# A graph layer on one core: records staged four units at a time, tags made relative on ScalarE

## The chip, the cores and the metric

The kernel runs on one core of a Trainium2 chip. The metric is the device time of one execution in microseconds. Before the change three runs gave 1980.95 to 1990.22 us, median 1985.97.

## What is computed

100,000 nodes with 128 features, 50,000 edges sorted by destination, 4 edge types:

```python
h = relu(layernorm(x))
for t in range(4):                       # message of an edge, by its type
    m_t = relu(concat(h[src], h[dst]) @ W1[t] + b1[t]) @ W2[t] + b2[t]
agg = segment_sum(where(edge_type == t, m_t, 0), dst)
r = sigmoid(agg @ Wir + bir + h @ Whr + bhr)
z = sigmoid(agg @ Wiz + biz + h @ Whz + bhz)
n = tanh(agg @ Win + bin + r * (h @ Whn + bhn))
out = x + (1 - z) * n + z * h
```

## The kernel before

The program is one software pipeline of 218 steps that all five engines walk through, each in its own order, with semaphores between them. A step carries work of two kinds.

**Edges.** 392 columns of 128 edges are sorted by type: a column's records (source, destination, place) are scattered to a table `lists` in DRAM, two columns (a unit) per step. Step i handles unit i + 9 of the 196 units. `stage_records` (L497 to L501) on GpSimd first copies a unit's records, 6 numbers a partition, from the big tile `records` into a slot of `stage` (8 slots), because the DMA's offsets are read there; `scatter` (L506) issues two indirect DMAs. `gather` (L513) then issues four indirect DMAs that fetch 128 rows of x each for list part q = i (204 parts). Between them stands the gate (L519), a 1x1 addition on GpSimd that all of a step's DMAs follow: its waits are for the staged copy (`l_staged`), for the rows' numbers that SyncE loaded from `lists` (`l_loaded`, L399) and for `e_normed`, by which a slot of `e_x` is free. A step of GpSimd is: copy, gate, two scatters, four gathers. SyncE loads a part's row numbers only when the scatters of the unit six further have landed.

Gathered rows get their layernorm statistics on VectorE (L799) one step later, are normalised on ScalarE seven steps after the gather (`e_h`, L998), turned and multiplied on TensorE, and end as messages with a tag: column 256 of a message holds the destination node's number (L949). ScalarE stores them to `messages` in DRAM (L1038) ten steps after the gather.

**Nodes.** 196 groups of 512 nodes. Group g is at work in steps g + 18 to g + 22. SyncE loads eight windows of 64 messages (L473) into a slot of `n_win` (4 slots), when the store of part g + 7 has landed. VectorE makes the selection matrix `n_sel` from them: four tensor_scalar operations (L906) of 128x256, each comparing node numbers with tags. TensorE sums the messages with it (L1207), ScalarE and VectorE split the sum in a high and a low part (L1077, L934), TensorE forms the gates' products (L1131 to L1133) and the rest is elementwise work: `n_r`, `n_n`, `n_zc` on ScalarE, `n_t`, `n_d`, `n_e`, `n_out` on VectorE. `n_sel` was

```python
for k in range(4):
    ins = V.tensor_scalar(n_sel[:, s % 2, k, :], iota[:], base[:, bass.ds(2 * g + k // 2, 1)],
                          n_win[:, s, k, TAG:ROW].bitcast(F32), ALU.add, ALU.is_equal)
```

with `iota` 0 to 255, `base` the first node number of each half group (392 columns, made once at L659) and the tag; both come from a tile, one number per partition.

The order in ScalarE's step is: three of four `e_h`, `n_r`, the fourth `e_h`, the store of messages, `e_ht`, `n_h_hi`, `n_a_hi`, one of four `n_h` (L1013), the store of the result and the load of x (L1051, L1030), `e_r` (L1089), two `n_h`, `n_n`, `n_zc`, one `n_h`, `e_msg`. VectorE's is: `n_out`, the message's low part (L896), `n_sel`, four statistics of edges, `n_t`, `n_xh` (L925), `n_h_lo`, `n_a_lo`, `n_t` again, four statistics of nodes (L807), the tag, `n_d`, `n_e`, with the links of a reciprocal square root between them. Each order is written out by hand in the engine's `step`; steps 0 to 31 and those from 184 are unrolled, the others run in a loop of eight.

## Time and profile before

| | before |
|---|---|
| median of 3 runs | 1985.97 us (1980.95 to 1990.22) |
| profiled execution | 1990.46 us, span 1988.6 us |
| VectorE (DVE) busy | 1791.4 us, 90% of the span |
| TensorE (PE) busy | 1748.1 us, 88% |
| ScalarE (ACT) busy | 1512.9 us, 76% |
| GpSimd (POOL) busy | 1356.8 us, 68% |
| granted TensorE clock | 0.995 |

The shares are means over stages: the first 230 us hold no node work, and scatters end near 1720 us. Busy time of GpSimd holds its DMA instructions but not the gaps between them. "issue" as what ended an idle time means that no semaphore of the profile did. An instruction's mean duration can overlap the next one's; the busy time of a group is a union.

### The profile page before, as it was taken

What the parts mean: (1) busy time and instruction counts of PE and PEld (TensorE: products, weight loads), DVE (VectorE), ACT (ScalarE), POOL (GpSimd) and SP (SyncE); (2) the same over time, 40 slices, a digit from 0 to 9 for tenths busy, and PEclk for the clock granted to TensorE, in tenths of its full rate; (3) what the DMA queues carried; (4) which work ended last, traced back from release to release, by engine and by line L of the source; (5) the groups of instructions that cost most, each with busy time, mean ns of one, the idle gap of its engine ahead of it and who ended that gap; (6) DMA issues with size and microseconds to landing.
All of it is one profiled execution on the core that took longest, in us unless ns stands there. A gap on an engine that the chain in (4) does not pass through costs nothing.

```text
span 1988.6 us, 45047 instructions
## 1 busy us (share of the span) xinstructions
PE 1748.1 (88%) x10146; PEld 1433.2 (72%) x10146; DVE 1791.4 (90%) x5325; ACT 1512.9 (76%) x3401; POOL 1356.8 (68%) x1644
## 2 busy tenths in 40 slices
PE   1015699999999999999999999999999999999898
PEld 0014477778877878788888888887887887788787
DVE  5434499999999999999999999999999999899897
ACT  0013588888888888888888888888888888788785
POOL 3777777777777777777777777777777777654300
PEclk9999999999999999999999999999999999999999
DMA  2224699988998999999999999999999999778853
GB/s 61 27 33 86 114 170 169 180 180 176 178 173 180 175 175 175 182 181 171 187 184 169 187 177 175 189 176 177 184 171 185 185 174 180 169 181 169 158 142 97
DMA packets 486059, 318.09 MB, mean 160 GB/s; under 512 B 117275, under 2 KB 472547, under 8 KB 485990
## 3 DMA queue, kind: packets, MB, share of 16 engines
q1 hardware_dynamic: 185286, 106.73, 37.6%
q10 hardware_dynamic: 261792, 156.12, 28.4%
q0 software_dynamic: 38912, 54.48, 16.1%
q14 instruction: 46, 0.38, 0.1%
q8 instruction: 23, 0.38, 0.1%
HBM read 211.39 MB, written 105.71 MB: 159 GB/s over the span
## 4 chain that ended last, share of the span: by engine, by line
PE 31%; POOL 27%; issue 15%; DVE 11%; DMA 5%; ACT 2%; SPq 1%; ACTq 1%; POOLq 0%; DVEq 0%
POOL e_x L513 16%; POOL lists L506 8%; PE bank L1131 6%; PE bank L1132 5%; PE bank L1133 5%; PE bank L1207 5%; DVE n_sel L906 3%; DMA n_win<-messages 2%; PE bank L1236 2%; DMA messages<-e_msg 2%; POOL gate_word L519 2%; PE bank L1218 2%; PE bank L1219 2%; PE bank L1246 2%; SPq L473 1%
## 5 line engine op out<-in xcount | busy, mean ns | idle before, releaser
L513 POOL DMA_INDIRECT e_x<-in_x,rows_now x816 | 826.2, 1012 | 253.1 <-issue 252.8
L506 POOL DMA_INDIRECT lists<-stage x392 | 402.2, 1026 | 144.8 <-issue 144.7
L998 ACT ACTIVATE e_h<-e_x,shift,rstd 128x128 f32<-128x128 f32 x816 | 354.0, 487 | 120.9 <-DVE shift L883 120.9
L1013 ACT ACTIVATE n_h<-n_x,shift,rstd 128x128 f32<-128x128 f32 x784 | 360.7, 487 | 0.0
L906 DVE TENSOR_SCALAR n_sel<-iota,base,n_win 128x256 fp32r<-128x256 f32 x784 | 275.0, 412 | 18.7 <-DMA n_win<-messages 18.5
L799 DVE BATCH_NORM_STATS2 bn<-e_x 128x6 f32<-128x128 f32 x816 | 175.9, 275 | 126.0 <-DMA e_x<-in_x,rows_now 125.3
L1207 PE MATMUL bank<-n_sel,n_win 128*128 128x256 f32 x1568 | 239.8, 296 | 45.3 <-DVE n_sel L906 43.4
L1131 PE MATMUL bank<-n_h_hi,whh_hi 128*128 128x512 f32 x588 | 248.3, 422 | 13.2 <-ACT n_zc L1101 5.6
L1207 PEld LDWEIGHTS bank<-n_sel,n_win 128*128 128x128 f32 x1568 | 199.3, 190 | 82.2 <-DVE n_sel L906 69.7
L1131 PE MATMUL bank<-n_a_hi,wih_hi 128*128 128x512 f32 x588 | 249.3, 424 | 0.0
L1133 PE MATMUL bank<-n_a_hi,wih_lo 128*128 128x512 f32 x588 | 233.4, 397 | 0.0
L1132 PE MATMUL bank<-n_a_lo,wih_hi 128*128 128x512 f32 x588 | 233.1, 396 | 0.0
L1133 PE MATMUL bank<-n_h_hi,whh_lo 128*128 128x512 f32 x588 | 232.3, 395 | 0.0
L1132 PE MATMUL bank<-n_h_lo,whh_hi 128*128 128x512 f32 x588 | 232.3, 395 | 0.0
L1187 PE MATMUL bank<-ident,e_h 128*128 128x128 f32 x816 | 127.8, 281 | 115.7 <-ACT e_h L998 114.8
L1077 ACT ACTIVATE n_a_hi<-bank 128x512 fp32r<-128x512 f32 x196 | 117.2, 598 | 144.4 <-PE bank L1207 136.1
L1089 ACT ACTIVATE e_r<-bank,b_cols 128x128 f32<-128x128 f32 x408 | 127.6, 364 | 108.8 <-DVE n_xh L925 55.2
L1187 PEld LDWEIGHTS bank<-ident,e_h 128*128 128x128 f32 x816 | 105.3, 145 | 142.4 <-issue 115.2
L1218 PE MATMUL bank<-e_ht,w 128*128 128x128 f32 x816 | 165.2, 286 | 34.4 <-DVE e_msg L896 30.9
L807 DVE BATCH_NORM_STATS2 bn<-n_x 128x6 f32<-128x128 f32 x784 | 167.9, 273 | 0.0
L1219 PE MATMUL bank<-e_ht,w 128*128 128x128 f32 x816 | 164.8, 285 | 0.0
L1218 PEld LDWEIGHTS bank<-e_ht,w 128*128 128x128 f32 x816 | 131.0, 200 | 37.5 <-issue 37.5
(141 smaller groups left out, 3879.4 us busy)
## 6 DMA issues: line engine op xcount, KB each, us to landing
n_win<-messages SPq DMA_DIRECT2D x1568, 64.2 KB
messages<-e_msg ACTq DMA_DIRECT2D x204, 257.0 KB
n_x<-in_x ACTq DMA_DIRECT2D x195, 256.0 KB
out<-n_out ACTq DMA_DIRECT2D x195, 256.0 KB
e_x<-in_x,rows_now POOLq DMA_INDIRECT x816
lists<-stage POOLq DMA_INDIRECT x392
rows_now<-lists SPq DMA_DIRECT2D x204, 2.0 KB
w<-in_W SPq DMA_DIRECT2D x1, 512.0 KB
```

What stands on the lines that cost most here:

```text
L506: G.indirect_dma_start(lists, bass.IndirectOffsetOnAxis(ap=stage[:, s, k, 2:3], axis=0), stage[:, s, k, 0:2], None).then_inc(l_scattered[s ...
L513: G.indirect_dma_start(e_x[:, s, 2 * end + t, :], None, x, bass.IndirectOffsetOnAxis(ap=rows_now[:, s, t, end:end + 1], axis=0)).then_inc( ...
L906: ins = V.tensor_scalar(n_sel[:, s % 2, k, :], iota[:], base[:, bass.ds(2 * g + k // 2, 1)], n_win[:, s, k, TAG:ROW].bitcast(F32), ALU.add ...
L998: last = A.activation(e_h[:, s % 2, k, :], e_x[:, s, k, :], ACT.Relu, scale=rstd[:, slot, col + k:col + k + 1], bias=shift[:, slot, col + ...
L1013: last = A.activation(n_h[:, s % 2, cols], n_x[:, s, cols], ACT.Relu, scale=rstd[:, slot, col + 4 + k:col + 5 + k], bias=shift[:, slot, co ...
L1131: T.matmul(o, w_hi, v_hi, start=start, stop=False)
L1132: T.matmul(o, w_hi, v_lo, start=False, stop=False)
L1133: return T.matmul(o, w_lo, v_hi, start=False, stop=stop)
L1187: last = T.transpose(bank[BE0][:, k * P:(k + 1) * P], e_h[:, s, k, :], ident[:])
L1207: last = T.matmul(o, n_win[:, w, k, part_ * D:(part_ + 1) * D], n_sel[:, s, k, :], start=n == 0, stop=n == 3)
L1218: T.matmul(o, w1[:, kind, 0, :], e_ht[:, s, t * P:(t + 1) * P], start=True, stop=False)
L1219: last = T.matmul(o, w1[:, kind, 1, :], e_ht[:, s, (2 + t) * P:(3 + t) * P], start=False, stop=True)
```

## The change

Two edits. GpSimd copies four units' records in one copy of 24 numbers a partition, into four slots, at the end of a step behind its gathers, in one step of four (and 0 and 4 ahead of the first scatter, 8 behind the first scatters); the gates of the other steps no longer wait for `l_staged`. In the loop the copy has no wait for earlier scatters of its slots. And ScalarE makes `n_rel` = tag - base at the head of its step, two activations of two columns, which takes over the wait for the windows (`n_windowed`); VectorE waits for `n_reled` and compares `iota` with `n_rel` alone. `base` is now made negative once. Nothing else is changed.

```diff
+        n_rel = sb("n_rel", [P, 2, 4])
...
             def stage_records(u, m):
                 s = m % UNROLL
-                if due(u - 7):
-                    pool.wait_ge(l_scattered[s], uses(u - 8, s, UNROLL, 32))
-                G.tensor_copy(stage[:, s, :, :], records[:, bass.ds(2 * u, 2), :]).then_inc(l_staged, 1)
+                if isinstance(u, int) and u >= UNROLL:
+                    for k in range(4):
+                        pool.wait_ge(l_scattered[s + k], uses(u - 8 + k, s + k, UNROLL, 32))
+                G.tensor_copy(stage[:, s:s + 4, :, :].rearrange("p u k c -> p (u k) c"),
+                              records[:, bass.ds(2 * u, 8), :]).then_inc(l_staged, 4)
...
-            for u in range(scatters_before(0)):
+            for u in (0, 4):
                 stage_records(u, u)
             for u in range(scatters_before(0)):
-                pool.wait_ge(l_staged, u + 1)
+                if u % 4 == 0:
+                    pool.wait_ge(l_staged, u + 4)
                 scatter(u, u)
+            stage_records(8, 8)
...
             def step(i, m):
-                for u, k in units:
-                    stage_records(u, k)
...
                 for u, k in units:
-                    pool.wait_ge(l_staged, u + 1)
+                    if k % 4 == 0:
+                        pool.wait_ge(l_staged, u + 4)
                 transfers_may_start(i + 1)
                 for u, k in units:
                     scatter(u, k)
                 if within(i, UNITS):
                     gather(i, m)
+                for u, k in units_of(i + 1, m + 1):
+                    if k % 4 == 0 and due(u - 7):
+                        stage_records(u, k)
...
-                link(V.tensor_copy(base[:], base_i[:]))
+                V.tensor_scalar(base[:], base_i[:], -1.0, None, ALU.mult).then_inc(s_bases, 1)
...
-                    dve.wait_ge(n_windowed[s], uses(g, s, 4, 128))
+                    dve.wait_ge(n_reled, g + 1)
...
-                        ins = V.tensor_scalar(n_sel[:, s % 2, k, :], iota[:], base[:, bass.ds(2 * g + k // 2, 1)],
-                                              n_win[:, s, k, TAG:ROW].bitcast(F32), ALU.add, ALU.is_equal)
+                        ins = V.tensor_scalar(n_sel[:, s % 2, k, :], iota[:], n_rel[:, s % 2, k:k + 1], None, ALU.is_equal)
...
             def step(i, m):
+                g, s = i - LAG + 1, (m - LAG + 1) % 4
+                if within(g, NG):
+                    if isinstance(g, int) and g == 0:
+                        act.wait_ge(s_bases, 1)
+                    act.wait_ge(n_windowed[s], uses(g, s, 4, 128))
+                    if due(g - 1):
+                        act.wait_ge(n_seled, g - 1)
+                    for half in range(2):
+                        rows = slice(2 * half, 2 * half + 2)
+                        last = A.activation(n_rel[:, s % 2, rows], n_win[:, s, rows, TAG].bitcast(F32), ACT.Identity,
+                                            bias=base[:, bass.ds(2 * g + half, 1)])
+                    last.then_inc(n_reled, 1)
                 normalise_edges(i, m, (0, 1, 2))
```

GpSimd's order in steps of its loop was, one step after the other:

```order
L501 COPY stage<-records 128x6 [waits l_scattered5]
L519 TENSOR_TENSOR gate_word<-g_power 1x1 [waits l_staged,l_gated,e_normed,l_loaded4]
L506 DMA lists<-stage 102400x2 x2
L513 DMA e_x<-in_x,rows_now 128x128 x4
L501 COPY stage<-records 128x6 [waits l_scattered6]
L519 TENSOR_TENSOR gate_word<-g_power 1x1 [waits l_staged,l_gated,e_normed,l_loaded5]
```

and is now:

```order
L507 COPY stage<-records 128x24 [waits l_scattered6,l_scattered5,l_scattered7,l_scattered4]
L526 TENSOR_TENSOR gate_word<-g_power 1x1 [waits l_staged,l_gated,e_normed,l_loaded3]
L513 DMA lists<-stage 102400x2 x2
L520 DMA e_x<-in_x,rows_now 128x128 x4
L526 TENSOR_TENSOR gate_word<-g_power 1x1 [waits l_gated,e_normed,l_loaded4]
L513 DMA lists<-stage 102400x2 x2
L520 DMA e_x<-in_x,rows_now 128x128 x4
L526 TENSOR_TENSOR gate_word<-g_power 1x1 [waits l_gated,e_normed,l_loaded5]
```

The copy of three gates is gone, and with it their wait for `l_staged`; in front of the fourth a copy of 24 numbers still stands, with nothing between it and the gate.

ScalarE's order from the end of one step into the next (ISA is a register operation on its queue) was:

```order
L1108 ACTIVATE e_msg<-bank 128x2x128 [waits e_tagged,e_messaged]
L987 ISA
L998 ACTIVATE e_h<-e_x,shift,rstd 128x128 [waits e_turned,ln_ops]
L998 ACTIVATE e_h<-e_x,shift,rstd 128x128 x2
L1061 ACTIVATE n_r<-bank,bsum 128x512 [waits n_ted,n_gate_r]
L998 ACTIVATE e_h<-e_x,shift,rstd 128x128 [waits ln_ops]
L1038 ISA [waits e_low]
L1038 DMA messages<-e_msg 128x2x257
```

and is now:

```order
L1131 ACTIVATE e_msg<-bank 128x2x128 [waits e_tagged,e_messaged]
L1070 ISA
L1075 ISA [waits n_seled,n_windowed0]
L1075 ACTIVATE n_rel<-n_win,base 128x2
L1075 ISA
L1075 ACTIVATE n_rel<-n_win,base 128x2
L998 ISA
L1009 ACTIVATE e_h<-e_x,shift,rstd 128x128 [waits e_turned,ln_ops]
L1009 ACTIVATE e_h<-e_x,shift,rstd 128x128 x2
L1084 ACTIVATE n_r<-bank,bsum 128x512 [waits n_ted,n_gate_r]
```

The wait for the windows stands ahead of all of ScalarE's step, and two activations with it.

## Rows read from the trace of the kernel before

**Rows 1.** Stretches: time, busy us (x instructions) by engine, clock, DMA share, GB/s
```profile
900.00:1650.00 750.00, 736.40 (x4349) 603.71 (x4348) 742.36 (x2217) 644.08 (x1447) 572.81 (x681) 1.00 0.94 180
1730.00:1825.00 95.00, 92.95 (x554) 76.61 (x554) 93.47 (x283) 81.59 (x184) 46.41 (x55) 1.00 0.76 178
```

**Rows 2.** Grouped lines, 900 to 1650 us: count, busy us, mean ns, idle before
```profile
L906 DVE TENSOR_SCALAR n_sel<-iota,base,n_win 128x256 fp32r<-128x256 f32 x340 | 119.5, 413 | 0.0
L1089 ACT ACTIVATE e_r<-bank,b_cols 128x128 f32<-128x128 f32 x170 | 53.2, 364 | 44.5 <-DVE n_xh L925 27.3 <-issue 17.2
L1077 ACT ACTIVATE n_a_hi<-bank 128x512 fp32r<-128x512 f32 x86 | 51.4, 598 | 54.4 <-PE bank L1207 53.8 <-issue 0.6
L1108 ACT ACTIVATE e_msg<-bank 128x256 fp32r<-128x256 f32 x85 | 31.5, 371 | 0.0
L519 POOL TENSOR_TENSOR gate_word<-g_power 1x1 f32<-1x1 f32 x85 | 30.6, 359 | 13.2 <-POOL stage L501 12.3
L501 POOL COPY stage<-records 128x6 int32 x86 | 28.0, 326 | 0.4
```

**Rows 3.** Waits, 400 to 1700 us: who, for whom, us, times, longest
```profile
POOL gate_word L519 <- ACT e_h L998: 6.8, 4, 2.9
DVE n_sel L906 <- DMA n_win<-messages: 5.8, 4, 2.4
...
DVE bn L799 <- DMA e_x<-in_x,rows_now: 0.2, 1, 0.2
```

**Rows 4.** Waits, 0 to 300 us
```profile
DVE bn L799 <- DMA e_x<-in_x,rows_now: 123.8, 18, 30.0
```

**Rows 5.** Timeline of GpSimd ahead of the loop: start, duration, instruction
```profile
27.85 2.12 POOL L501 COPY stage<-records 128x6 int32<-128x6 int32 x7 [24.69 <-DVE records L644]
30.15 1.49 POOL L506 DMA_INDIRECT lists<-stage  x1 [0.17 <-POOL stage L501]
...
180.49 0.19 POOL L501 COPY stage<-records 128x6 int32<-128x6 int32 x1
180.92 0.19 POOL L519 TENSOR_TENSOR gate_word<-g_power 1x1 f32<-1x1 f32 x1 [0.24 <-POOL stage L501]
...
189.42 0.18 POOL L519 TENSOR_TENSOR gate_word<-g_power 1x1 f32<-1x1 f32 x1 [0.24 <-POOL stage L501]
```

**Rows 6.** Grouped lines of VectorE, 3 to 5 us
```profile
L608 DVE CAST iota<-iota_i 128x256 f32<-128x256 int32 x1 | 0.3, 295 | 0.0
L609 DVE TENSOR_SCALAR above_r<-iota,part 128x128 fp32r<-128x128 f32 x1 | 0.3, 285 | 0.0
...
L610 DVE CAST ones_r<-ones 128x128 fp32r<-128x128 f32 x1 | 0.2, 220 | 0.0
```

**Rows 7.** Timeline of a step of the loop, all engines
```profile
1012.54 0.39 ACTq L1038 DMA_DIRECT2D messages<-e_msg  x1
...
1014.89 0.20 POOL L501 COPY stage<-records 128x6 int32 x1
...
1015.25 0.82 POOL L519 TENSOR_TENSOR gate_word<-g_power 1x1 f32<-1x1 f32 x1 [0.17 <-POOL stage L501]
...
1016.84 5.27 SPq L473 DMA_DIRECT2D n_win<-messages  x8
...
1018.86 0.98 POOL L513 DMA_INDIRECT e_x<-in_x,rows_now  x1 [0.30 <-issue]
...
1019.90 1.26 ACT L998 ACTIVATE e_h<-e_x,shift,rstd 128x128 f32<-128x128 f32 x3
...
1021.13 1.37 DVE L906 TENSOR_SCALAR n_sel<-iota,base,n_win 128x256 fp32r<-128x256 f32 x4
...
1021.38 0.38 ACTq L1038 DMA_DIRECT2D messages<-e_msg  x1
```

**Rows 8.** The chain of waits, 520 to 580 us: start, duration, what
```profile
540.43 7.41 DMA messages<-e_msg
...
553.11 6.08 DMA n_win<-messages
```

More of the change, by code:

```diff
@@ L279, in gnn_layer @@
         s_edges_ready = sem("s_edges_ready")
+        s_bases = sem("s_bases")
         g_blank = sem("g_blank")
@@ L333, in gnn_layer @@
         n_xhed = sem("n_xhed")
+        n_reled = sem("n_reled")
         n_seled = sem("n_seled")
@@ L548, in _, with units_of @@
             pool.wait_ge(s_spots, 1)
-            for u in range(scatters_before(0)):
+            for u in (0, 4):
                 stage_records(u, u)
             for u in range(scatters_before(0)):
-                pool.wait_ge(l_staged, u + 1)
+                if u % 4 == 0:
+                    pool.wait_ge(l_staged, u + 4)
                 scatter(u, u)
+            stage_records(8, 8)
             pool.wait_ge(s_iota, 1)
             G.tensor_tensor(gate_word[:, 0:1], g_power[0:1, 0:1], g_power[0:1, 0:1], ALU.add).then_inc(l_gated, 1)
+            def units_of(i, m):
+                if not isinstance(i, int):
+                    return [(i + LEAD, m + LEAD)]
+                return [(u, u) for u in range(scatters_before(i), min(scatters_before(i + 1), SCATTERS))]
             def step(i, m):
-                units = []
-                if not isinstance(i, int):
-                    units = [(i + LEAD, m + LEAD)]
-                else:
-                    units = [(u, u) for u in range(scatters_before(i), min(scatters_before(i + 1), SCATTERS))]
-                for u, k in units:
-                    stage_records(u, k)
+                units = units_of(i, m)
                 if within(i, UNITS):
```

## The prediction

> **What bounds the kernel now.** I read the stretches first. From 900 to 1650 us VectorE is busy 742.4 of 750 us and TensorE 736.4; ScalarE has 644.1 and GpSimd 572.8 [rows 1]. A count of the grouped lines turns this into steps: 85 gates of GpSimd in that stretch, so 750/85 = 8.82 us a step, and VectorE is busy 8.73 of them [rows 1, 2]. The waits from 400 to 1700 us say whose busy time is real: VectorE waits for a window of messages 4 times (5.8 us) and once for gathered rows (0.2 us) in some 147 steps, so it waits for nobody [rows 3]. TensorE's busy time is modelled and proves less. When the scatters end, GpSimd falls to 46.4 of 95 us and VectorE still has 93.5 [rows 1]: VectorE's own work sets the step there, not what GpSimd takes from it.
>
> GpSimd looks free by its busy time and is not. In its sequence nearly each DMA instruction has 0.30 us in front of it that no semaphore ends (the gather at 1018.86 [rows 7]); I take that as part of the instruction. It waits for e_normed, its only brake, 4 times (6.8 us) [rows 3]. So it also works through its 8.82 us. Two engines are level, and a change on one alone would give little. Before 300 us GpSimd leads alone: VectorE waits 123.8 us for gathered rows, 18 times [rows 4], and a step takes 189.42 - 180.92 = 8.50 us [rows 5].
>
> **VectorE: a pointer scalar less.** n_sel is 128x256, two [P,1] operands, 413 ns, four a step [rows 2]. What the second pointer costs no row tells alone. Without a pointer a 128x128 cast takes 220 ns, with one a 128x128 tensor_scalar takes 285: 65 ns for a pointer; without one 128x256 takes 295 [rows 6]. One pointer on 256 columns would then be 360, against 413 for two, and the second would cost 53; were the two equal, 59. From below: 0, if both are loaded together and 413 is 295 plus one lot of 118. From above: 413 - 295 = 118, if what is left costs nothing. I take 57, between these two. 4 x 57 = 0.23 us a step; of it I count 0.22, since such ops overlap. VectorE's step goes from 8.82 to 8.60. The constant's sign (a tensor_scalar in place of a cast, once) costs nothing that counts: it is done before VectorE waits for its first gathers.
>
> The Trainium skill (VectorE: DVE Perf Modes, the TRN2 errata) gives a VectorE op on SBUF as 58 cycles and the columns over the mode's factor, with no term for pointers. By it n_sel costs the same with one as with two, this term is 0 and the time is that of the rival of the free pointer; the 285 ns on 128 columns beside 295 on 256 speak against it.
>
> **GpSimd: three copies of four go.** In the steady stretch copy and the wait behind it are 28.0 + 13.2 us over 85 steps, 0.48 a step; undisturbed they are 0.36 (1014.89 to 1015.25) [rows 2, 7]. Before the loop they are 0.43 (180.49 to 180.92) [rows 5]. What takes their place in a step without a copy is the gate right behind a DMA, 0.05 at a guess between 0 and 0.30. I take 0.36 saved in three steps of four, 0.27 a step. In the fourth, the copy still stands directly in front of its gate (nothing lies between "behind the gathers" and the next step's head), and has 24 columns for 6: saving 0. The copy's waits for four scatters hold nothing: they are four to eight steps old. Seven copies before the first scatter, 2.12 us and 0.17 [rows 5], become two, and a third stands behind the first scatters: 1.2 us saved. GpSimd's step: 8.82 - 0.27 = 8.55, and 8.50 - 0.28 at the start.
>
> **ScalarE: two small activations at the head.** A pair of e_r with a bias pointer is 53.2/85 = 0.63 us for 128 columns [rows 2]; two columns must be less, and it can't be below 0. An n_a_hi of 512 columns takes 598 ns and an e_msg of 256 takes 371 [rows 2], 0.89 ns a column, so 126 columns fewer leave about 0.15 of each half of the 0.63; with a step's register work I take 0.35 for both. ScalarE idles before n_a_hi and e_r 54.4 + 44.5 us over 85 steps, 1.16 a step [rows 2]; that is the cover, and without it 0.35 would be on the path. The Trainium skill (ScalarE: Activation LUTs, what ACT_TABLE_LOAD costs) makes it 188 ns apiece, 0.38 for both: the cover holds by either.
>
> What waits now at ScalarE's head is n_windowed, and behind it e_h, n_r, the store of messages and e_ht are queued; VectorE waits for n_reled as it did for the window. The head is 1.23 us before n_sel (1019.90 against 1021.13) [rows 7], so windows have that much less time. In the trace a store issued at 1012.54 lets SyncE go at 1016.84, and its eight loads take 5.27 us, to 1022.11; the ScalarE head that needs them comes at 1019.90 + 8.82 = 1028.7 [rows 7]. That leaves 6.6 us for landing; shorter steps and the later store take 0.8 of it, 5.8. A late load took 6.08 us after a store of 7.41 [rows 8]. So now and then the head waits; I give 3 us back in all for it.
>
> **The sum.** Steady: 192 of the 196 steps with node work x 0.22 = 42 us. Start, where GpSimd leads: 17 of the first 23 steps have no copy, x (0.43 - 0.05) = 6, and 1.2: 7 us. Back: 3. Together 46 less. The profiled execution took 1990.5 us (span 1988.6), the median run 1986.0, so I start from their middle, 1988.2: **1942 us**. Against the profiled time alone it would be 1944.5, against the median 1940.
>
> **Rivals.**
> *GpSimd becomes the bound (chance 0.21).* If only 0.17 a step goes on average, because what VectorE's operations block is blocked elsewhere (a gate took 0.82 us at 1015.25 under n_xh, where 0.18 is usual [rows 5, 7]), GpSimd's step is 8.65 to 8.70 and VectorE waits for gathers at last. 0.14 x 192 = 27, and 6: 1988 - 33 = 1955. For it: it is level now. Against: n_sel holds less long. The Trainium skill (SBUF — State Buffer, who interferes with whom) says that a tensor_scalar in a two-port mode locks GpSimd out for the whole instruction, and that two SBUF inputs block its reads; the gate of 0.82 us under an addition of two SBUF tiles agrees.
>
> *The second pointer is free (0.12).* Then VectorE keeps 8.82, and only the start is gained: 1981. For it: only 128-column ops show what a first pointer costs, none a second. This is also how the change would fail to do what it says.
>
> *The window becomes the bound at ScalarE's head (0.07): slower.* The store goes out 1.48 us behind the head (1019.90 to 1021.38 [rows 7]), 1.83 with the two activations. The head of two steps on waits for it, so a step is at least (trip + 1.83)/2, the trip being store issue to last landing. Here it is 4.30 + 5.27 + landing; with 6.08 it is 15.65 and the step 8.74, hidden under 8.82 but not under 8.60. From a mean trip of 15.9 (step 8.87) the kernel is slower than before. DMA queues are 94% busy at 180 GB/s [rows 1], and a faster step loads them more; at 16.1 the step is 8.97, and 0.15 x 192 = 29, less 7 of the start: 1988 + 22 = 2010. Against: VectorE waited for windows four times in 147 steps.
>
> **How the numbers follow.** The forecast has 0.60. Its own range is 1925 to 1960: the low end takes 0.29 a step (n_sel at 340 ns, and less blocking) and gives nothing back, the high end 0.14. GpSimd as the bound lies in it or just above. The range, 1922 to 1982, takes in the free pointer and leaves out the window rival and a gain from the full 118 ns. 0.5%, 10 us, is what a measurement can tell from no change. Faster by over that (below 1976): forecast, GpSimd rival, and a little of the rest, 0.81. Within: the free pointer and a mild window case, 0.12. Slower: 0.07.
>
> **What the profile after would show.** n_sel at 350 to 360 ns; VectorE still busy 99% with 8.6 us from gate to gate. If n_sel is at 400 or more, the VectorE term is wrong. Copies of 128x24, some 49, right in front of every fourth gate, and other gates within 0.1 us of the last gather. If VectorE's bn waits for gathers in the steady stretch, GpSimd is the bound. If ScalarE shows tens of us of waits for n_win at n_rel, and VectorE then waits for n_rel, it is the window; the prediction is wrong if those waits pass 20 us, or if the step isn't below 8.7.

## The result and the profile after

The changed kernel takes 1962.6 us in the median of six runs (1955.7 to 1973.0), the kernel before 1981.7 us in the median of six (1979.9 to 1990.2). The ratio is 0.9897, with a 95% interval of 0.987 to 0.9924: about 1.0% faster, 19 us. The prediction said 46 us. The profiled execution took 1973.0 us, the longest of the six, with a span of 1971.2; I compare it with the profiled one of before (1990.5, span 1988.6, also the longest of its six), 17.4 us apart. In what follows, a ratio with an interval compares undisturbed runs only, while a median is that of all runs.

Busy time and a group of instructions from the page of the changed kernel (columns as in the rows ahead of the prediction):

```profile
PE 1735.8 (88%) x10146; PEld 1436.8 (73%) x10146; DVE 1768.0 (90%) x5325; ACT 1545.4 (78%) x3793; POOL 1307.9 (66%) x1497
...
L918 DVE TENSOR_SCALAR n_sel<-iota,n_rel 128x256 fp32r<-128x256 f32 x784 | 248.9, 379 | 24.2 <-ACT n_rel L1075 23.7
```

The two stretches of [rows 1], for the changed kernel:

```profile
900.00:1650.00 750.00, 729.36 (x4328) 603.50 (x4327) 731.57 (x2202) 654.35 (x1613) 544.47 (x615) 1.00 0.90 179
1730.00:1825.00 95.00, 93.44 (x551) 77.71 (x550) 92.15 (x286) 83.75 (x206) 42.80 (x52) 0.98 0.77 174
```

VectorE has lost 10.8 us of busy time in 750 and stands idle for 18.4 us there instead of 7.6 [rows 1]. The grouped lines of the same stretch, which answer to [rows 2]:

```profile
L526 POOL TENSOR_TENSOR gate_word<-g_power 1x1 f32<-1x1 f32 x85 | 17.8, 210 | 34.8 <-ACT e_h L1009 31.0 <-POOL stage L507 3.3
L507 POOL COPY stage<-records 128x24 int32 x21 | 4.5, 216 | 0.1
...
L1112 ACT ACTIVATE e_r<-bank,b_cols 128x128 f32<-128x128 f32 x170 | 53.1, 364 | 43.6 <-DVE n_xh L936 24.6 <-issue 17.5 <-PE bank L1242 1.2
L1100 ACT ACTIVATE n_a_hi<-bank 128x512 fp32r<-128x512 f32 x85 | 50.8, 597 | 37.8 <-PE bank L1230 36.9 <-issue 0.8
...
L1075 ACT ACTIVATE n_rel<-n_win,base 128x2 f32<-128x2 f32 x170 | 40.7, 290 | 13.7 <-DMA n_win<-messages 13.6
...
L1131 ACT ACTIVATE e_msg<-bank 128x256 fp32r<-128x256 f32 x85 | 31.5, 371 | 0.0
```

GpSimd's copies and gates now cost 22.3 us instead of 58.6 [rows 2], but what it gained it waits out: its gate waits 31.0 us for ScalarE's e_h. The waits from 400 to 1700 us, against [rows 3]:

```profile
POOL gate_word L526 <- ACT e_h L1009: 52.5, 75, 4.0
...
ACT n_rel L1075 <- DMA n_win<-messages: 27.4, 13, 3.6
...
DVE n_sel L918 <- ACT n_rel L1075: 14.7, 10, 2.8
```

Windows were waited for 4 times (5.8 us) before [rows 3] and are 13 times now (27.4 us), at ScalarE's head, and half of that reaches VectorE. Such a trip in the chain of waits (start, duration, what), beside [rows 8]:

```profile
1068.13 7.40 DMA messages<-e_msg
...
1080.30 6.55 DMA n_win<-messages
```

And the start, in GpSimd's timeline, against [rows 5]:

```profile
27.88 0.77 POOL L507 COPY stage<-records 128x24 int32<-128x24 int32 x2 [24.71 <-DVE records L656]
28.82 1.53 POOL L513 DMA_INDIRECT lists<-stage  x1 [0.17 <-POOL stage L507]
...
154.42 0.21 POOL L507 COPY stage<-records 128x24 int32<-128x24 int32 x1
154.88 0.18 POOL L526 TENSOR_TENSOR gate_word<-g_power 1x1 f32<-1x1 f32 x1 [0.24 <-POOL stage L507]
155.57 1.03 POOL L513 DMA_INDIRECT lists<-stage  x1 [0.52 <-issue]
...
162.09 1.02 POOL L520 DMA_INDIRECT e_x<-in_x,rows_now  x1 [0.30 <-issue]
163.14 0.18 POOL L526 TENSOR_TENSOR gate_word<-g_power 1x1 f32<-1x1 f32 x1
163.48 1.01 POOL L513 DMA_INDIRECT lists<-stage  x1 [0.16 <-POOL gate_word L526]
...
170.84 0.18 POOL L526 TENSOR_TENSOR gate_word<-g_power 1x1 f32<-1x1 f32 x1
```

A step without a copy takes 170.84 - 163.14 = 7.70 us, against 8.50 [rows 5]. The copy and its wait are gone (0.43), and so is most of the pause behind the gate (0.36 of 0.52): the first scatter comes 0.16 us behind a gate that waited for nothing, 0.52 behind one that waited. The first row operation (n_sel) stands at 220.7 us instead of 233.3.

**Where the 17.4 us come from.** I took the start of each step's first n_sel from both traces. The first is 12.6 us earlier, the last 17.2 (1954.6 against 1971.8). So the start gave 12.6 us, the 195 steps behind it 4.5, and the rest 0.2. The 4.5 are not spread evenly: the 17th n_sel group stands at 361.4 us against 381.8, a lead of 20.3 us, and from there to the last the changed kernel loses 3 us again. Behind 382 us it gained nothing in these two executions. The steps of a calm stretch repeat in eights:

```
step time us, first n_sel to first n_sel, eight steps of a calm stretch          mean
before  8.43  8.91  9.01  8.75  8.49  9.01  9.02  8.75                            8.80
after   8.39  8.91  8.78  8.68  8.59  8.99  8.83  8.68                            8.73
```

Calm steps are only 0.07 us shorter (70.37 against 69.85 for the eight), where 0.22 was predicted. Over all 195 steps, those up to 9.2 us last 8.77 us in the mean before (181 of them) and 8.66 after (171), which gives 21.7 us; the longer ones exceed that mean by 28.3 us together before (14) and by 45.4 after (24), which takes back 17.1. So there are two questions: why is the calm step hardly shorter, and are the long steps a cost of the change?

The long steps, sorted by what VectorE waits for in them: those with a wait of n_sel for its windows, and the ones right behind them, make up 21.9 us before (12 steps) and 28.8 after (17), 6.9 more. The rest are 6.4 us before (2 steps) and 16.7 after (7), 10.3 more. Five of these seven follow each other from 1679.7 to 1738 us, without a wait for windows. There VectorE waits for TensorE's and ScalarE's results, and the granted clock is 0.88:

```profile
1679.00:1738.00 59.00, 49.41 (x261) 41.16 (x261) 44.46 (x136) 41.41 (x101) 25.68 (x31) 0.88 0.65 149
```

The kernel before has one such step, of 14.3 us at 1698.6. Whether the change has a part in these five is not shown.

### The profile page after: what moved, and what is told of

The parts are those of the page before. It is cut to its first block, busy times and chain, and to the rows that moved or that the text cites. A ratio compares the mean times of both kernels' runs of the same rounds, so it can differ in the third digit from the quotient of the medians.

```text
span 1971.2 us, 45215 instructions
## 1 busy us (share of the span) xinstructions
PE 1735.8 (88%) x10146; PEld 1436.8 (73%) x10146; DVE 1768.0 (90%) x5325; ACT 1545.4 (78%) x3793; POOL 1307.9 (66%) x1497
## 4 chain that ended last, share of the span: by engine, by line
PE 49%; DVE 16%; DMA 9%; issue 8%; ACT 4%; SPq 3%; POOL 2%; ACTq 1%; DVEq 0%; POOLq 0%
PE bank L1154 9%; PE bank L1156 8%; PE bank L1155 8%; PE bank L1230 7%; DMA messages<-e_msg 5%; DMA n_win<-messages 4%; DVE n_sel L918 4%; PE bank L1259 4%; SPq L476 3%; PE bank L1241 3%; PE bank L1242 3%; PE bank L1269 2%; DVE bn L811 2%; PE bank L1210 2%; PE bank L1255 2%
## 5 line engine op out<-in xcount | busy, mean ns | idle before, releaser
L513 POOL DMA_INDIRECT lists<-stage x392 | 410.9, 1048 | 141.9 <-issue 139.5
L918 DVE TENSOR_SCALAR n_sel<-iota,n_rel 128x256 fp32r<-128x256 f32 x784 | 248.9, 379 | 24.2 <-ACT n_rel L1075 23.7
L1154 PE MATMUL bank<-n_h_hi,whh_hi 128*128 128x512 f32 x588 | 248.8, 423 | 17.4 <-ACT n_zc L1124 8.8
```

Of the source, the lines that this page charges most:

```text
L513: G.indirect_dma_start(lists, bass.IndirectOffsetOnAxis(ap=stage[:, s, k, 2:3], axis=0), stage[:, s, k, 0:2], None).then_inc(l_scattered[s ...
L918: ins = V.tensor_scalar(n_sel[:, s % 2, k, :], iota[:], n_rel[:, s % 2, k:k + 1], None, ALU.is_equal)
L1154: T.matmul(o, w_hi, v_hi, start=start, stop=False)
```

## What holds the calm step

From 1356 to 1636 us both traces are calm. The stretch, first before, then after (columns as in [rows 1]):

```profile
1356.00:1636.00 280.00, 275.07 (x1624) 225.09 (x1623) 277.33 (x827) 240.18 (x542) 211.41 (x255) 1.00 0.94 180
```

```profile
1356.00:1636.00 280.00, 273.49 (x1631) 225.90 (x1630) 275.46 (x831) 245.82 (x607) 204.29 (x231) 1.00 0.91 181
```

VectorE's n_sel in it, before and after:

```profile
L906 DVE TENSOR_SCALAR n_sel<-iota,base,n_win 128x256 fp32r<-128x256 f32 x127 | 44.9, 415 | 0.0
```

```profile
L918 DVE TENSOR_SCALAR n_sel<-iota,n_rel 128x256 fp32r<-128x256 f32 x128 | 42.1, 390 | 1.3 <-ACT n_rel L1075 1.3
```

In busy time (operations overlap) four n_sel are 4 x 44.9/127 = 1.41 us before and 4 x 42.1/128 = 1.32 after, 0.10 a step. (The 1.3 us of waiting are one wait, in a single long step.) Yet the operation itself is as short as predicted. The query of one line (duration minimum, median and maximum), from 900 to 1650 us, before and after:

```profile
L906 DVE TENSOR_SCALAR n_sel<-iota,base,n_win x340: 394/406/639, 906.6 to 1647.2; 128x256 fp32r<-128x256 f32 x170
```

```profile
L918 DVE TENSOR_SCALAR n_sel<-iota,n_rel x340: 333/347/562, 901.9 to 1645.6; 128x256 fp32r<-128x256 f32 x170
```

The median is 347 ns against 406, but the mean is 388 against 413: some operations are much longer than the rest. I set against each other when GpSimd's DMA instruction ends and how long the n_sel under way takes. In a timeline of the changed kernel:

```profile
1364.18 1.35 DVE L918 TENSOR_SCALAR n_sel<-iota,n_rel 128x256 fp32r<-128x256 f32 x4
...
1364.46 0.96 POOL L520 DMA_INDIRECT e_x<-in_x,rows_now  x1 [0.30 <-issue]
...
1365.70 0.18 POOL L526 TENSOR_TENSOR gate_word<-g_power 1x1 f32<-1x1 f32 x1 [0.28 <-ACT e_h L1009]
```

The last gather ends at 1365.42, the fourth n_sel at 1365.53, 0.11 us behind it; it took 551 ns. At 347 ns it would have ended 0.2 us earlier. Counted over all n_sel between 300 and 1900 us (worked out from the traces: the first end of a GpSimd DMA instruction behind the start of the n_sel, and how much longer than 413 or 346 ns the n_sel took):

```
DMA instruction ends      before (two pointers)      after (one pointer)
behind the start of       n_sel   over 30   mean     n_sel   over 30   mean
the n_sel by              met     ns more   extra    met     ns more   extra
0 to 250 ns                27       0        -6        8       0         0
250 to 300                 81       0        -6        2       2       +45
300 to 350                 23      14       +34       29      29      +100
350 to 400                 23      23       +71       31      31      +141
400 to 450                  5       5      +114       81      81      +201
450 to 500                  4       4      +168        3       2      +150
```

This is the shape of a wait: an n_sel whose own end falls near the end of a GpSimd DMA instruction ends some 110 ns behind it, and where its own end comes well before, it loses nothing. In the changed kernel all 143 met between 250 and 450 ns are late, in the kernel before all 28 met between 350 and 450. That 81 met between 250 and 300 lose nothing before fits too: the end of the DMA instruction and 110 ns is still under 413. Summed, such meetings cost 24 us after and 4 us before. That is 20 us over 180 steps, 0.11 a step, half of what the shorter operation should have given.

The steps up to 9.2 us between 400 and 1680 us close the sum (worked out from the traces, means in us):

```
                                   before   after   difference
step                                8.80    8.71       0.09
first n_sel's start to the          1.40    1.30       0.10
  fourth one's end
the same where no n_sel is late     1.37    1.13       0.24
```

So of 0.24 us, 0.14 go to late n_sel, and all the rest of the step is as long as before (7.40 us in both).

Other operations of VectorE serve as a control. Between 300 and 1900 us of the changed kernel, 60 n_sel have the end of a GpSimd DMA instruction within 90 ns ahead of to 50 ns behind the place where they would end undisturbed, and all 60 are late. 88 of the layernorm statistics and 57 n_a_lo have one there as well, and none is late: of the 1424 statistics none takes over 291 ns, with medians of 271 and 272. So the wait belongs to n_sel and not to VectorE as a whole.

Why are there more of them? Not because GpSimd has moved under n_sel. Between 300 and 1700 us a GpSimd DMA instruction ends 1.13 to 1.29 us behind the step's first n_sel in 82 of 158 steps before, and in 107 of 158 after. One of the 82, from the step of [rows 7], whose first n_sel starts at 1021.13:

```profile
1021.42 0.95 POOL L513 DMA_INDIRECT e_x<-in_x,rows_now  x1 [0.30 <-issue]
```

It ends at 1022.37, 1.24 us behind, and the four n_sel take 407 to 408 ns. What has moved is n_sel's own end. With two pointers the fourth runs from 0.97 to 1.38 us behind the first one's start, past 1.2 + 0.11. With one it would run from 0.80 to 1.14, and it ends at 1.30 in the median. The shorter operation draws its end to where the DMA instruction's end was all along. GpSimd's wait for e_h (the next gate comes 1.5 us behind the first n_sel in the median, 2.9 before) changes which gather lies there, the last one after and the one before it in the step shown. Why a DMA instruction ends there so often in both kernels is not shown.

## The experiments

Two theories were put down with the runs. **A**: the row operation waits for the end of GpSimd's DMA instruction, and this gives back VectorE's gain. **B**: the wait for windows, now at ScalarE's head, gives it back.

At about 1980 us neither half of the change was measured alone. Most runs came out in a condition that the first measurement did not have: on four chips the kernel before itself took 2639 to 2713 us in the median. Each is compared with the kernel before of its own set, but of the change at 1980 us these say little; they have a part of their own below. One set, on a fifth chip, came near the first measurement (the kernel before at 2021.6 us) and is told first.

### The light kernels: TensorE relieved, before and after

```diff
             def product(o, w_hi, w_lo, v_hi, v_lo, start, stop):
-                T.matmul(o, w_hi, v_hi, start=start, stop=False)
-                T.matmul(o, w_hi, v_lo, start=False, stop=False)
-                return T.matmul(o, w_lo, v_hi, start=False, stop=stop)
+                return T.matmul(o, w_hi, v_hi, start=start, stop=stop)
```

The same edit in the kernel before (l0) and in the changed one (l1). Expected of l0:

> The kernel before with TensorE relieved: each gate's product is its first matmul alone, so 12 of the 18 matmuls of 128x512 of a step are left out and with them the low parts of the product (part of the computation is left out). It tests two things. First, that the runs of 2640 to 2710 us were long because TensorE's results came late: every unexplained wait there stands before an operation that reads one of TensorE's banks. If so, this kernel takes 1900 to 2000 us although the kernel before takes 2600 us or more beside it; if the memory or the queues were slow, it takes 2400 us or more as well. Second, it is the base for the other light kernels: VectorE's 413 ns row operations and its step of 8.6 to 8.8 us hold it.

Expected of l1:

> The changed kernel with TensorE relieved in the same way (12 of 18 gate matmuls of a step left out). Against the light kernel before, if VectorE bounds both: with the row operations free of GpSimd the step would fall by the whole 0.24 us, to about 8.5, and the time by 45 to 60 us with the start. Theory A (a row operation that meets the end of a GpSimd DMA instruction waits for it) says that part of it is given back as in the full kernel: 60 or more delayed row operations between 900 and 1650 us, each ending some 110 ns behind the end of a GpSimd DMA instruction, calm step only 0.05 to 0.15 lower, 15 to 40 us in all. Theory B (the waits on windows at ScalarE's head) says calm steps lower by 0.2 and more, and the loss in single long steps behind a wait of ScalarE on windows.

**Measured.** l0 2026.0 us (2014.3 to 2041.3, 4 runs), l1 2003.4 us (1983.6 to 2020.7, 10 runs), the kernel before 2021.6 us (1984.4 to 2062.9, 13 runs). l0 is 1.0125 of the kernel before (0.993 to 1.032), l1 1.0006 (0.994 to 1.007); the light change from l0 to l1 is 22.6 us by the medians, in the 15 to 40 that theory A gave. With TensorE's busy time down to 523.6 of 750 us, l0 is no faster within its interval, and its calm steps are those of the kernel before. TensorE does not bound these steps, for all its 98% of busy time [rows 1]. The calm eight of l0 are 8.43, 8.90, 8.99, 8.74, 8.49, 8.97, 9.00, 8.75, those of the kernel before to 0.04; those of l1 are those of the changed kernel.

Theory A's count came out: 69 n_sel of l1 took over 50 ns too long between 900 and 1650 us (86 in the changed kernel) and lost 10.7 us, in the median 112 ns behind the end of a DMA instruction of GpSimd; 11 in l0, 0.9 us. Yet in l0 the next gate comes 1.6 us behind the first n_sel, nearly as early as in the changed kernel. So an early gate alone does not make n_sel late; the short operation does. The first n_sel stands at 221.1 us against 231.8: the start again, 10.7 us.

These two traces also hold a control. Behind 1790 us the scatters have ended, GpSimd's last gather is done over 2.6 us ahead of the next gate, and no DMA instruction ends near the end of an n_sel. The line query on five calm steps of l0, then of l1:

```profile
L906 DVE TENSOR_SCALAR n_sel<-iota,base,n_win x20: 403/406/411, 1815.2 to 1851.1; 128x256 fp32r<-128x256 f32 x20
```

```profile
L918 DVE TENSOR_SCALAR n_sel<-iota,n_rel x20: 342/347/350, 1800.4 to 1835.2; 128x256 fp32r<-128x256 f32 x20
```

No n_sel is late (at most 411 and 350 ns), and the steps are 8.31, 8.97, 8.88, 8.74 in l0 and 8.07, 8.73, 8.68, 8.50 in l1: 0.23 us a step, the whole of the predicted 0.22. Where the two engines do not meet, the step falls by what the operation lost. So the predicted term is real, and in the steady stretch meetings take back over half of it. (GpSimd has less to do there in other ways too, as its scatters are over.) The changed kernel's own stretch behind 1750 us reads the same, with four steps of 8.74, 8.68, 8.50 and 8.07 us against 8.44, 8.97, 8.88 and 8.75 in the kernel before, 0.26 a step:

```profile
L918 DVE TENSOR_SCALAR n_sel<-iota,n_rel x24: 342/345/348, 1754.8 to 1798.3; 128x256 fp32r<-128x256 f32 x24
```

Theory B is not gone with that. On this chip windows were late more often in both kernels. From 400 to 1700 us, first l0, then l1:

```profile
DVE n_sel L906 <- DMA n_win<-messages: 41.4, 19, 5.1
```

```profile
ACT n_rel L1075 <- DMA n_win<-messages: 78.2, 39, 5.9
...
DVE n_sel L918 <- ACT n_rel L1075: 46.6, 26, 4.9
```

The number of waits doubled, and yet VectorE lost about the same to them (46.6 against 41.4 us), and the steps over 9.2 us exceed the mean of the others by 93 us in l1 against 84 in l0. The earlier wait costs something, some 5 to 10 us here, and not the gain of the calm step, which B would have left at 0.2.

### Half of the change alone, n_sel moved, GpSimd shifted

Copies alone (the subtraction stays in n_sel), cut to its core:

```diff
-                    dve.wait_ge(n_reled, g + 1)
+                    dve.wait_ge(n_windowed[s], uses(g, s, 4, 128))
...
-                        ins = V.tensor_scalar(n_sel[:, s % 2, k, :], iota[:], n_rel[:, s % 2, k:k + 1], None, ALU.is_equal)
+                        ins = V.tensor_scalar(n_sel[:, s % 2, k, :], iota[:], base[:, bass.ds(2 * g + k // 2, 1)],
+                                              n_win[:, s, k, TAG:ROW].bitcast(F32), ALU.add, ALU.is_equal)
```

> The copies of four units alone; n_sel with two pointers and base on VectorE as before. Theory A (a VectorE operation of n_sel that meets the end of a GpSimd DMA instruction waits for it; GpSimd, being faster, is now held by e_normed at a fixed place where its last gather meets n_sel): first n_sel 12 us earlier than before, gates wait for e_h in the loop, the fourth n_sel is longer than the others by 50 ns or more, the loop's step is 8.79 to 8.95 as before or longer; 1970 to 1985 us. Theory B (the wait for windows at ScalarE's head takes the gain; port meetings don't matter): step 8.79, few waits for windows, 1972 to 1976 us.

Subtraction alone (one copy in front of each gate, as before):

```diff
-                for u, k in units_of(i + 1, m + 1):
-                    if k % 4 == 0 and due(u - 7):
-                        stage_records(u, k)
...
+                for u, k in units:
+                    stage_records(u, k)
```

> ScalarE's subtraction alone; copies as before. Theory A: no gain at the start, n_sel about 346 ns with few operations delayed as in the kernel before (GpSimd has no slack and so is not held at one place), step 8.60 to 8.70 in calm stretches unless GpSimd becomes the bound; 1955 to 1975 us. Theory B: n_rel waits for windows 25 us or more between 400 and 1700 us as in the changed kernel, and the total is 1980 or more.

All four n_sel behind the edge statistics (late), and two of the four there (split):

```diff
+                last = None
+                if within(i - 1, UNITS):
+                    last = edge_stats(i - 1, m - 1)
                 g, s = i - LAG + 1, (m - LAG + 1) % 4
                 if within(g, NG):
                     dve.wait_ge(n_reled, g + 1)
```

> The changed kernel with n_sel behind the four statistics of edges on VectorE, 0.8 us later in the step. Theory A: operations of n_sel no longer meet the last gather's end; delayed ones fall from 86 in 750 us to under 40, and the step falls by 0.1 unless TensorE, which gets n_sel later, becomes the bound; 1940 to 1965 us. Theory B: VectorE's waits for n_rel fall, ScalarE's for windows stay; no other change, 1955 to 1962 us.

```diff
-                    for k in range(4):
+                    for k in (0, 1):
...
+                if within(g, NG):
+                    for k in (2, 3):
+                        ins = V.tensor_scalar(n_sel[:, s % 2, k, :], iota[:], n_rel[:, s % 2, k:k + 1], None, ALU.is_equal)
+                    ins.then_inc(n_seled, 1)
```

> The changed kernel with two of the four n_sel ahead of the statistics of edges and two behind them, and TensorE starting on the first half. The end of the last gather falls in the statistics, which do not use the port. Theory A: nearly no delayed n_sel, calm step 8.73 to 8.60, 1935 to 1955 us. Theory B: as the changed kernel, 1958 to 1966 us.

Three of them were repeated, since the kernel before itself was slow beside them:

> Only the copies of four units on GpSimd; the tags' subtraction stays in VectorE's operation with two pointers. The same kernel as e1_copies, run again because the kernel before itself took some 2700 us beside e1_copies, so that no part of the change could be read there. What is expected with the kernel before at about 1980 us: the start is shorter by the whole 12 us (first row operation of L914's place at 221 us instead of 233), and the steady step stays at about 8.79, since VectorE keeps its 413 ns operations and holds it. Both theories give 1968 to 1975 us, ratio 0.993 to 0.997.

> Only ScalarE's subtraction and VectorE's operation with one pointer; GpSimd copies one unit before each gate as before. The same kernel as e2_rel, run again for the same reason. Theory A (the shorter operations meet the end of a GpSimd DMA instruction): GpSimd's step of 8.50 and more now leaves still less room below VectorE's, so GpSimd's gates and DMA instructions lie against the row operations as they do in the changed kernel or closer: step 8.70 to 8.80, 1970 to 1982 us, ratio 0.994 to 1.000. Theory B (the wait for windows at ScalarE's head takes the gain, the calm step is 8.60): waits of ScalarE on windows of 25 us and more and a calm step of 8.65 or less, 1965 to 1975 us.

> Only ScalarE's subtraction and VectorE's operation with one pointer; GpSimd copies one unit before each gate as in the kernel before. The same kernel as e2_rel. The first row operation should stand at 231 to 234 us, as in the kernel before, since the start is GpSimd's. Theory A: GpSimd's DMA instructions lie against the row operations as closely as in the changed kernel, calm step 8.68 to 8.80, 40 or more delayed operations; with a start that gains nothing the ratio to the kernel before is 0.994 to 1.002. Theory B: calm step 8.65 or less and waits of ScalarE on windows of 25 us and more, ratio 0.988 to 0.995. Against the changed kernel's 0.990, the difference is what the copies of four units bring.

> The changed kernel with two of the four row operations of VectorE moved behind the next edge statistics. The same kernel as e4_split, run again because the kernel before itself took some 2700 us beside it. With the kernel before at about 1980 us, theory A: two of the four operations lie elsewhere against GpSimd's DMA instructions, so the fourth is no longer met by the last gather in each step: fewer than 60 delayed operations between 900 and 1650 us (86 in the changed kernel) and a calm step of 8.60 to 8.70, 1945 to 1960 us. Theory B: the waits on windows stay at some 25 us, the step stays at 8.7, 1958 to 1970 us.

> The changed kernel with two of the four row operations of VectorE moved behind the next edge statistics; the same kernel as e4_split, now hoped for beside a kernel before of about 1980 to 2020 us (on the chip of the light kernels the kernel before took 2021.6 us). Theory A: the fourth operation is no longer met by the last gather in each step: fewer than 60 delayed operations between 900 and 1650 us (86 in the changed kernel), calm step 8.60 to 8.70 instead of 8.73, and 0.5 to 1.5% below the changed kernel's 0.990 of the kernel before, so a ratio of 0.975 to 0.985. Theory B: waits on windows decide, the calm step is 8.73 or the same within 0.03, ratio 0.987 to 0.995.

And GpSimd's DMA instructions shifted against VectorE:

```diff
+                pool.wait_ge(l_gated, i + 1)
+                for n in range(2):
+                    G.tensor_tensor(pad[:, n:n + 1], g_power[0:1, 0:1], g_power[0:1, 0:1], ALU.add)
                 transfers_may_start(i + 1)
```

> The changed kernel with two small GpSimd additions of one element (some 0.19 us each) before each gate, which move GpSimd's eight DMA instructions of a step 0.4 to 0.5 us later against VectorE's operations; nothing else changes. With the kernel before at about 1980 us: theory A (a row operation that meets the end of a GpSimd DMA instruction waits for it) says that the calm step changes, because other row operations are met: 8.60 to 8.75 if the last gather now ends behind the four row operations or between them and another, and operations are delayed at other positions than the fourth; GpSimd's own sequence takes about 0.45 us a step more and still fits under 8.7. Theory B (waits for windows at ScalarE's head) says no change of the calm step, 8.73, and the same ends within 0.3%. If the kernel before takes some 2700 us again, TensorE's late results bound every step, GpSimd waits several us in most steps, and both theories say no difference from the changed kernel.

**Measured**, each beside the kernel before of its own set (medians in us; without an interval the ratio is that of the medians):

```
                    this      before    this/before
copies alone      e1  2709.8    2697.5    1.005
                  e1b 2730.7    2712.9    1.007
subtraction alone e2  2611.4    2697.5    0.9705  (0.961 to 0.980)
                  e2b 2611.3    2712.9    0.955   (0.940 to 0.970)
                  e2c 2562.7    2655.1    0.968   (0.953 to 0.984)
n_sel late        e3  2776.0    2697.5    1.033   (1.023 to 1.042)
n_sel split       e4  2649.9    2697.5    0.982
                  e4b 2554.1    2639.0    0.973   (0.963 to 0.983)
                  e4c 2539.3    2655.1    0.962   (0.953 to 0.972)
GpSimd shifted    e5  2567.9    2639.0    0.973
```

None of these expectations' times could be put to the test, since all assumed 1980 us. Of their counts, those of the late and split kernels came out (4, and 7 to 12 delayed n_sel), and the 40 or more of the subtraction alone did not (22 to 35). What the sets say is this.

**The condition itself.** Steps take 11 to 13 us, the granted clock from 900 to 1650 us is 0.86 to 0.91 in the mean (1.00 is the level of 2.4 GHz, 0.5 that of 1.2) instead of 1.00 in [rows 1], and all engines pause. A stretch of e2c (columns as in [rows 1]):

```profile
900.00:1650.00 750.00, 599.03 (x3236) 488.14 (x3237) 553.11 (x1649) 494.67 (x1205) 411.54 (x506) 0.91 0.76 133
```

Its waits from 400 to 1700 us:

```profile
POOL gate_word L522 <- ACT e_h L1000: 354.2, 94, 10.3
ACT n_r L1075 <- remote: 133.9, 52, 3.5
...
PE bank L1221 <- DVE n_sel L909: 68.9, 29, 4.6
DVE n_out L895 <- remote: 68.1, 30, 4.1
...
ACT n_rel L1066 <- DMA n_win<-messages: 6.5, 2, 4.2
```

"Remote" is a release that the trace cannot assign. In each of the ten traces of this condition, from 300 to 1900 us, it stands before n_r, n_out, n_t, n_zc, e_msg, e_r, e_ht, n_a_hi and n_h_hi and before nothing else, and each of these reads a bank that TensorE has written; in the traces of before and after the change and in the light ones it does not occur. That points at TensorE's results coming late, by up to 10.4 us; what held them the trace does not tell. The light kernels were to show whether TensorE is the cause, but beside them the kernel before took 2021.6 us: the condition was not there, and the test not made. The lower clock alone is not enough: from 1023.7 to 1031 us in e2b the granted clock is 1.00, the gate matmuls start 0.23 us apart, and n_r then waits 1.7 us all the same (waits of e2b, 1030 to 1033 us):

```profile
ACT n_r L1075 <- remote: 1.7, 1, 1.7
```

The cause stays open.

**What the parts do there.** TensorE waits for n_sel 46 to 91 us between 400 and 1700 us in each of these traces, against 21.4 in the kernel before at 1990 us. Where it waits, n_sel would be on the path, and its time would count in another way; this is argued from the waits and not tested. The subtraction alone gains 3 to 4.5%; all four n_sel moved behind 0.86 us of statistics lose 3%, against the subtraction alone some 0.8 us a step ((2776 - 2611)/196); and the copies alone gain nothing that can be seen, as they relieve an engine that waits 455 us for e_h anyway (e1b, 400 to 1700 us). So in that condition the gain that was measured is the subtraction's; the changed kernel itself was not run there.

**What they say on A.** The late kernel moves n_sel away from the last gather. From 900 to 1650 us, by the same line query:

```profile
L922 DVE TENSOR_SCALAR n_sel<-iota,n_rel x236: 333/346/524, 900.6 to 1647.5; 128x256 fp32r<-128x256 f32 x118
```

Four of these 236 took over 50 ns too long; in the split kernel 7 to 12 did, and where n_sel stayed in its place (e2, e2b, e2c, e5) 22 to 35. The ends again lie some 105 to 115 ns behind the DMA instruction in the median. In e2c all 54 n_sel met between 300 and 450 ns behind their start were late, by 110, 145 and 207 ns in the three slots of the table, as in the changed kernel (100, 141, 201), though the two kernels keep quite another pace. That supports A's mechanism. The shifted GpSimd (e5) tells nothing on the calm step it was made for, as there was none: 22 of its n_sel were late, as in e2. Which place of n_sel is best at 1980 us was not tried: the split kernel is no better than the subtraction alone in the first set (2650 against 2611) and ahead by less than the spread of the runs in the third (2539 against 2563).

## Why the prediction was wrong in its size

The direction was right, and 1962.6 us lies in the range, but the forecast of 1942 (its own range 1925 to 1960) missed by 20 us. That it lies in the range is partly luck: the start gained 5.6 us more than predicted, while the steps behind it gained far less.

- **VectorE's term, 42 us, is the step that failed.** The size of the operation was right: 347 ns in the median where 350 to 360 stood, the second pointer 59 ns. What failed is "of it I count 0.22" a step: that the whole of a shorter operation reaches the step. Steps up to 9.2 us fell by 0.09 between 400 and 1680 us, since 0.14 of the 0.24 goes to n_sel waiting for the end of GpSimd's DMA instructions. Over all 195 steps it was 0.11 a step, 21.7 us where 42 were forecast. Where nothing meets, the full 0.23 shows.
- **GpSimd's start, 7 us, was 12.6.** The term mis-sized is the saving in a step without a copy: 0.38 predicted, 8.50 - 7.70 = 0.80 measured, because the pause behind the gate fell as well (0.52 to 0.16), which no row of before could show, each gate there having waited, for a copy or, at the end, for e_normed. The 1.2 us of the first copies came as 2.12 - 0.77 = 1.35. By 17 such steps and the first copies it would be 15 us, and the gate of the 23rd step does stand 15.5 us earlier (242.4 against 257.9).
- **GpSimd's steady term** took nothing from the end, as predicted: the gate's wait for e_h went from 6.8 us [rows 3] to 52.5.
- **ScalarE's cost** was 40.7/85 = 0.48 us busy a step, for 0.35 predicted. The prediction's own figures give more than it took: half of 0.63 less 126 columns of 0.89 ns is 0.20 for each activation, not 0.15. The idle time in front of n_a_hi and e_r fell from 98.9 [rows 2] to 81.4 us, and the rest of the calm step did not grow, so it was covered.
- **Windows, 3 us back**, were 27.4 us of waits at ScalarE's head, over the 20 that the prediction named as proving it wrong, and 14.7 at VectorE. The step did not come below 8.7 in the mean either, the other such sign: 8.73 in the calm eight, 8.84 from 900 to 1650 us with the long ones. In steps longer than 9.2 us the windows cost 6.9 us more than before, and the two light kernels put it at 5 to 10. The rival itself (the window holds each step, 2010 us) did not come: the calm step never waits.
- **No term at all** stood for the other long steps: 10.3 us more than before in these two executions, mostly the five from 1679.7 us. Their cause stays open. With it the sum closes: 12.6 + 21.7 - 6.9 - 10.3 = 17.1, and the last n_sel stands 17.2 us earlier.
- **Rival "GpSimd becomes the bound"** gave 1955 us by its number and fails by its mechanism: VectorE never waits for gathers in the steady stretch. Its reason was that the engines block each other. They do, but what took the gain is VectorE's side of it. The gate of 0.82 us at 1015.25 [rows 7] was the other direction; gates are 210 ns in the mean after, 359 before [rows 2]. The Trainium skill (SBUF — State Buffer, who interferes with whom) says that whichever of the two issues first gets the shared pair of ports for its whole instruction, and the other blocks. The trace agrees that VectorE can be the one that waits, but not on the whole instruction: an n_sel met by the end of a DMA instruction of 0.95 us within 250 ns of its start ran under it and lost nothing (0 of 8 late after, 0 of 27 before).
- **Rival "the second pointer is free"** is out: 347 against 406 ns. The formula of the Trainium skill (VectorE: DVE Perf Modes, TRN2 errata) has no term for pointers, and by it the two would cost the same; the trace does not agree.

## What to carry to other kernels

When two engines run level, a saving on one is not free of the other: before counting it, look for what ends near the place where the shortened instruction will end. Compare the median and the mean of an operation's duration; a mean well over the median (347 and 388 here) says that some wait inside, and the time since the neighbour's last end says for what. And a busy share proves a bound only with the waits: TensorE at 98% was no bound of the calm step, as taking two thirds of its gate matmuls away showed.

## What was not expected of the hardware

- An n_sel of VectorE whose own end falls near the end of a GpSimd DMA instruction ends about 110 ns behind it, losing up to some 200 ns; one that ends earlier loses nothing, and of 1424 statistics of VectorE in the same trace none lost any.
- GpSimd's next DMA instruction starts 0.16 us behind a gate that waited for nothing and 0.52 us behind one that waited.
- A pair of activations of 128x2 takes 0.48 us, though one of 128x256 takes 371 ns.
- On four chips the same kernel before took 2639 to 2713 us instead of 1982, with unassigned waits of up to 10.4 us before readers of TensorE's banks and a granted clock of 0.86 to 0.91. Times are to be compared within a set only.
